# Two graph layers with norms on one core: the step loop of every engine becomes straight code with constant waits

## The reference

```python
def _L0_gnn_ref(input_graph, adj, Wq, bq, Wk, bk, Wv, bv, beta):   # 12 heads of 32
    q, k, v = split(x @ Wq + bq), split(x @ Wk + bk), split(x @ Wv + bv)
    scores = einsum('bhqd,bhkd->bhqk', q, k) / sqrt(HD) + beta * adj
    scores = where(adj > 0, scores, -9e15)
    return merge(einsum('bhqk,bhkd->bhqd', softmax(scores), v))

def layer(h, params):                                              # two of these
    u = einsum('bid,bjd->bij', h, h) / sqrt(D)
    delta = softmax(u) * adj
    attn = delta / (sum(delta) + 1e-10)
    hl, hs, hr = h @ wl.T + b_l, h @ ws.T + b_s, h @ wr.T + b_r
    ctx = (attn * upper) @ hl + diag(attn) * hs + (attn * lower) @ hr
    return relu((ctx - mean) / sqrt(var + 1e-12) * g + beta)

x = layernorm(x + attention(x, adj))
x = layernorm(x + layer(layer(x)))
```

## Time and profile before

| | |
|---|---|
| median of 3 runs | 1378.46 us (1377.25 to 1379.92) |
| profiled execution, its own time | 1381.73 us |
| span of that execution (first to last instruction) | 1380.0 us |
| granted clock of TensorE, mean over the span | 0.982 of full speed |
| PE busy | 1313.9 us, 95% |
| DVE busy | 1057.1 us, 77% |
| ACT busy | 757.1 us, 55% |
| POOL busy | 597.1 us, 43% |

### The profile page before, as it was taken

One profiled execution on the slowest core, in us unless ns is written; L12 is line 12 of the kernel. 1 busy time (PEld: TensorE's weight loads), 2 busy tenths in 40 slices (PEclk: granted clock), 3 DMA queues, 4 the chain that ended last, 5 costly groups with the idle time before them and its releaser, 6 DMA issues.

```text
span 1380.0 us, 37486 instructions
## 1 busy us (share of the span) xinstructions
PE 1313.9 (95%) x13568; PEld 1289.9 (93%) x13568; DVE 1057.1 (77%) x2665; ACT 757.1 (55%) x1579; POOL 597.1 (43%) x656
## 2 busy tenths in 40 slices
PE   3799999999999999999999999999999999999895
PEld 3799999999999999999999999999999999999884
DVE  3358877878877888887787887788888778787765
ACT  4355555565555565555555555556555556555553
POOL 1344444444444444444444445444444444444432
PEclk9799999999999999999999999999999999999997
DMA  7210111110011111011111011111101111101000
GB/s 243 78 40 2 51 51 52 52 50 19 30 50 50 50 50 40 9 50 50 50 50 50 19 31 50 50 50 50 39 11 50 50 50 50 50 15 26 25 13 24
DMA packets 49445, 62.74 MB, mean 45 GB/s; under 512 B 14320, under 2 KB 35952, under 8 KB 49392
## 3 DMA queue, kind: packets, MB, share of 16 engines
q1 hardware_dynamic: 49392, 62.03, 14.7%
HBM read 36.44 MB, written 12.58 MB: 36 GB/s over the span
## 4 chain that ended last, share of the span: by engine, by line
PE 94%; DMA 2%; issue 1%; DVE 1%; ACT 1%; POOL 0%; SPq 0%; POOLq 0%; ACTq 0%
PE bank L315 26%; PE bank L317 25%; PE bank L316 25%; PE bank L427 4%; PE bank L393 4%; PE bank L378 3%; PE bank L364 3%; PE bank L414 2%; PE bank L404 2%; DMA late<-in_w 2%; PE bank L455 1%; ACT w_hi L520 0%; DVE ln_six L841 0%; DVE w_lo L683 0%; ACT late L621 0%
## 5 line engine op out<-in xcount | busy, mean ns | idle before, releaser
L315 PE MATMUL bank<-w_hi,hT_hi 128*128 128x384 f32 x1152 | 403.0, 350 | 9.6 <-issue 9.2
L316 PE MATMUL bank<-w_lo,hT_hi 128*128 128x384 f32 x1152 | 390.8, 339 | 0.0
L317 PE MATMUL bank<-w_hi,hT_lo 128*128 128x384 f32 x1152 | 390.6, 339 | 0.0
L997 POOL TENSOR_TENSOR hlr_lo<-late,hlr_hi 128x384 fp32r<-128x384 f32 x256 | 240.5, 940 | 245.8 <-ACT hlr_hi L596 244.4
L596 ACT ACTIVATE hlr_hi<-late 128x384 fp32r<-128x384 f32 x256 | 134.5, 526 | 222.3 <-DVE late L798 220.4
L315 PEld LDWEIGHTS bank<-w_hi,hT_hi 128*128 128x128 f32 x1152 | 217.2, 189 | 15.3 <-issue 12.4
L798 DVE TENSOR_TENSOR late<-bank,rows 128x384 f32<-128x384 f32 x256 | 142.1, 555 | 101.9 <-PE bank L317 97.9
L316 PEld LDWEIGHTS bank<-w_lo,hT_hi 128*128 128x128 f32 x1152 | 217.6, 189 | 0.0
L317 PEld LDWEIGHTS bank<-w_hi,hT_lo 128*128 128x128 f32 x1152 | 217.1, 188 | 0.0
L1010 POOL TENSOR_TENSOR ln_rstd<-ln_var,minus_half 128x2 f32<-128x2 f32 x128 | 98.7, 771 | 225.1 <-DVE ln_var L867 117.4
L315 PE MATMUL bank<-xT_hi,w_hi 128*128 128x256 f32 x576 | 164.6, 286 | 8.4 <-ACT kT L535 8.4
(11 more groups left out here) (93 smaller groups left out, 2804.7 us busy)
## 6 DMA issues: line engine op xcount, KB each, us to landing
v_halves<-v_stage SPq DMA_DIRECT2D x128, 99.0 KB, 2.3
xT_in<-in_xT SPq DMA_DIRECT2D x32, 384.0 KB, 3.1
x_in<-in_x SPq DMA_DIRECT2D x32, 384.0 KB, 3.8
out<-late SPq DMA_DIRECT2D x32, 384.0 KB, 2.4
late<-in_w SPq DMA_DIRECT2D x9, 576.0 KB, 6.1
adj_in<-in_adj SPq DMA_DIRECT2D x32, 64.0 KB, 3.5
adjT_in<-in_adjT SPq DMA_DIRECT2D x64, 32.0 KB, 2.9
rows<-in_bl SPq DMA_DIRECT2D x2, 192.0 KB, 6.2
```

What stands on the lines that cost most here:

```text
L315: nc.tensor.matmul(o, l_hi, r_hi, start=n == 0, stop=False)
L316: nc.tensor.matmul(o, l_hi, r_lo, start=False, stop=False)
L317: done = nc.tensor.matmul(o, l_lo, r_hi, start=False, stop=n == last)
L997: nc.gpsimd.tensor_tensor(hlr_lo[:, t, m, 0:D], hlr[:, t, m], hlr_hi[:, t, m, 0:D].bitcast(F32), ALU.subtract).then_inc(hlrlo_ready, 1)
```

## The change

All 35 steps are emitted one after the other on every engine; there is no loop, no register and no branch. Each wait is for a constant. The helper `need_alone` is replaced by `need`, so the extra waits on `consts_set` are gone; SyncE's wait on `v_staged`, which the loop body left out, now stands in every step. The arithmetic, the order of the operations on each engine and all buffers are the same.

```diff
-    def __init__(self, it, par):
-        self.it, self.par, self.fixed = it, par, isinstance(it, int)
+    def __init__(self, s):
+        self.s = s
...
     def count(self, stage, per, k):
 
-        const = (self.par + stage) * per + k
-        if self.fixed:
-            value = 2 * self.it * per + const
-            return value if value > 0 else None
-        assert LOOP_FROM * per + const > 0
-        return self.it * (2 * per) + const
+        value = (self.s + stage) * per + k
+        return value if value > 0 else None
...
-def steps(nc, engine, emit):
-    for s in range(-STAGES_BEFORE, LOOP_FROM):
-        emit(Step(s // 2, s % 2))
-    with nc.Fori(LOOP_FROM // 2, LOOP_TO // 2, engines=(engine,), hint_back_edge=True) as it:
-        emit(Step(it, 0))
-        emit(Step(it, 1))
-    for s in range(LOOP_TO, UNITS + STAGES_AFTER):
-        emit(Step(s // 2, s % 2))
+def steps(emit):
+    for s in range(-STAGES_BEFORE, UNITS + STAGES_AFTER):
+        emit(Step(s))
...
-        def need_alone(eng, st, sem, value):
-
-            if not st.fixed:
-                eng.wait_ge(consts_set, 1)
-            need(eng, sem, value)
...
                 if st.has(EARLY):
 
-                    if st.fixed:
-                        need(sp, v_staged, st.count(EARLY, 2, 2))
-                    need_alone(sp, st, o_scaled, st.count(MID, 2, 2))
+                    need(sp, v_staged, st.count(EARLY, 2, 2))
+                    need(sp, o_scaled, st.count(MID, 2, 2))
```

More of the change, by code:

```diff
@@ L9 @@
 ACT = mybir.ActivationFunctionType
-ENG = mybir.EngineType
 AX_X = mybir.AxisListType.X
@@ L41 @@
 class Step:
-    def __init__(self, it, par):
-        self.it, self.par, self.fixed = it, par, isinstance(it, int)
+    def __init__(self, s):
+        self.s = s
     def has(self, stage):
-        return not self.fixed or 0 <= 2 * self.it + self.par + stage < UNITS
+        return 0 <= self.s + stage < UNITS
     def unit(self, stage):
-        return self.it * 2 + (self.par + stage)
+        return self.s + stage
     def slot(self, stage):
-        return (self.par + stage) % 2
+        return (self.s + stage) % 2
     def count(self, stage, per, k):
-        const = (self.par + stage) * per + k
-        if self.fixed:
-            value = 2 * self.it * per + const
-            return value if value > 0 else None
-        assert LOOP_FROM * per + const > 0
-        return self.it * (2 * per) + const
-    def dma_count(self, stage):
[L67 to L72, removed]
-    def count_pair(self, stage):
[L76 to L80, removed]
+        value = (self.s + stage) * per + k
+        return value if value > 0 else None
+    def dma_count(self, stage):
+        value = 16 * ((self.s + stage) // 2 + 1)
+        return value if value > 0 else None
+    def count_pair(self, stage):
+        value = 32 * ((self.s + stage) // 2 + 1)
+        return value if value > 0 else None
 def need(eng, sem, value):
@@ L249, in load_xT @@
             def load_xT(st, ahead):
-                need_alone(sp, st, xlo_ready, st.count(ahead - 2, 1, 1))
+                need(sp, xlo_ready, st.count(ahead - 2, 1, 1))
                 slot = st.slot(ahead)
@@ L255, in load_x @@
                 slot = st.slot(ahead)
-                need_alone(sp, st, x_added, st.count(ahead - 2, 2, 2))
+                need(sp, x_added, st.count(ahead - 2, 2, 2))
                 sp.dma_start(x_in[:, slot], x[st.unit(ahead)]).then_inc(x_loaded[slot], 16)
@@ L283, in step @@
             def step(st):
-                if st.fixed and st.unit(EARLY) == 0:
+                if st.unit(EARLY) == 0:
                     for n in range(RAW, NW):
@@ L291, in step @@
                 if st.has(FINAL):
-                    need_alone(sp, st, y_ready, st.count(FINAL, 2, 2))
+                    need(sp, y_ready, st.count(FINAL, 2, 2))
                     sp.dma_start(out[st.unit(FINAL)], c1).then_inc(y_stored, 16)
                 if st.has(EARLY):
-                    if st.fixed:
-                        need(sp, v_staged, st.count(EARLY, 2, 2))
-                    need_alone(sp, st, o_scaled, st.count(MID, 2, 2))
+                    need(sp, v_staged, st.count(EARLY, 2, 2))
+                    need(sp, o_scaled, st.count(MID, 2, 2))
                     for g in range(GRAPHS):
@@ L303, in step @@
                             sp.dma_start(dst, src.rearrange("p t h d -> p t (h d)")).then_inc(v_moved, 16)
-            steps(nc, ENG.SP, step)
+            steps(step)
             sp.wait_ge(y_stored, 16 * UNITS)
@@ L435, in project_sides @@
             def project_sides(st, l):
-                if st.fixed and st.unit(LATE) == 0 and l == 0:
+                if st.unit(LATE) == 0 and l == 0:
                     pe.wait_ge(w_hi_set, NW)
@@ L507, in step @@
                     mix(st, 1)
-            steps(nc, ENG.PE, step)
+            steps(step)
         @block.scalar
@@ L673, in step @@
                     scale_self(st, 1)
-            steps(nc, ENG.Activation, step)
+            steps(step)
         @block.vector
@@ L691, in stats @@
                 for t in range(T):
-                    need_alone(dve, st, s_six, st.count(stage, per, k + t + 1))
+                    need(dve, s_six, st.count(stage, per, k + t + 1))
                     nc.vector.bn_aggr(mv[:, t], six[:, t]).then_inc(s_mv, 1)
@@ L716, in make_add @@
                 need(dve, adj_loaded[slot], st.dma_count(MID))
-                if st.fixed and st.unit(MID) == 0:
+                if st.unit(MID) == 0:
                     dve.wait_ge(cols_in, 80)
@@ L842, in stats_inner @@
                 for t in range(T):
-                    need_alone(dve, st, s_six, st.count(stage, 2, t + 1))
+                    need(dve, s_six, st.count(stage, 2, t + 1))
                     nc.vector.bn_aggr(mv[:, t], six[:, t]).then_inc(s_mv, 1)
@@ L933, in step @@
                     self_bias(st, 1)
-            steps(nc, ENG.DVE, step)
+            steps(step)
         @block.gpsimd
@@ L1037, in step @@
                     sides_low(st, 1, 1)
-            steps(nc, ENG.Pool, step)
+            steps(step)
 _SHAPE = (B, N, D)
```

1 line of the change is left out of this document (removed).

## The result

| | before | changed |
|---|---|---|
| median of 20 runs each, us | 1378.89 (1376.77 to 1380.72) | 1375.65 (1373.37 to 1376.86) |
| ratio | | 0.9977, 95% interval 0.9970 to 0.9984 |
| span of the profiled execution, us | 1380.0 | 1373.9 |

The changed kernel is faster by 0.23% (0.16% to 0.30%), 3.2 us of the 4.55 forecast. Of the changed kernel's page these lines answer to the earlier trace rows; the columns are the same.

The account below looks back on a forecast made before the run. PE, busy for 95% of the span, was taken to bound the kernel. Back edge 2.29, step 28 1.81 and step 29 0.45 sum to 4.55 us, off a median of 1378.46: 1373.9 us, range 1371.2 to 1377.8.

Parts of the forecast that it names:

- The back edge: Loop steps 4 to 27: POOL's late `xT_lo` holds up DVE, then PE; straight code gives back 2.29 us.
- The exit: Steps 28 and 29: engines leaving the loop reach code not yet fetched; without a loop 1.81 and 0.45 us go.
- Late fetches: Straight code from step 6 on adds about 124 fetch packets; cost between 0 and 87 us, taken as near 0.
- Costed at nothing: Register instructions inside the steps, waits on `consts_set` and SyncE's new wait for `v_staged`: claimed to cost no time.
- The slower rival: Steps 28 and 29 show straight code's true face, with late fetches throughout steps 4 to 27; 1403 us, chance 0.09.
- C: The slower rival's letter in the prediction: late fetches are the way of straight code; 1403 us, chance 0.09.

Follow-up runs that it names:

- the control: The kernel before, unchanged, run once more against itself; ratio 1.0006 (0.9997 to 1.0016).
- the shifted one: The changed kernel with 48 more instructions of satisfied waits at the start of PE's program; ratio to the kernel before 0.9975 (0.9963 to 0.9988).
- the version without that wait: The changed kernel with `make_add` moved behind `hT_low` and `max_gram` on DVE; medians 1368.94 and 1367.35 us, ratios to the kernel before 0.9938 and 0.9912.

## Why the prediction came out as it did

**The direction, the place and the shape** were right. The time of 1375.65 lies in the range of 1371.2 to 1377.8, and the gain is 0.7 of the forecast. A little of the closeness is luck: the forecast stood on a median of 1378.46 from three runs, and twenty runs gave 1378.89, which took 0.4 us off the miss.

**The back edge, 2.29 us.** The two traces of the loop give 979.25 and 979.02, the two of straight code 977.20 and 977.09, so 2.0 us: the term was 0.3 too large. The mechanism was right in its main part: `xT_lo` late, DVE behind it, PE behind DVE. The run with `make_add` late shows it, since the price vanishes with the loop still in place. Incomplete was my account of why `xT_lo` is late. I named POOL's register wait alone. It is 0.09 of the 0.15 us; the other 0.06 is ACT's back edge ahead of `xT_hi`. That the lateness passes on one for one is what the rows show: `xT_lo` 0.15 us later, PE's idle time 0.16 us longer.

**The exit, 1.81 + 0.45 = 2.26 us.** This is the term that was mis-sized. That it belongs to the exit and goes as a whole is shown (the loop to step 16, PE alone, ACT and DVE alone). Its size was read from one execution. Against 40.71 it is 2.26 there, 1.29 in the control, and 1.72 where the loop ends at 16. The mean of the three is 1.76. The run on POOL alone, which left the exit as it was, has 1.89, and the two loops with `make_add` late have 1.90 and 1.75 over their own steps. The prediction read the largest of six. Where the surplus lies is seen too: PE's gap in the scores was 1.02 us there and 0.47 to 0.75 in the others, and DVE's gap of 0.25 us in step 29 is in two traces (before, and POOL alone) and absent in the control, with PE alone and in step 17 of the loop to 16. The reading of step 28 was also incomplete. The two idle times make 1.51 of the 1.81 us; the other 0.3 is PE's busy time, 41.01 for 40.51, less the usual wait of 0.21 before the first product, which falls away.

**Late fetches.** I put their cost near 0, and it is: 0.05 + 0.16 us in one trace, and in the other a delay of 0.08 that a wait took up. I had no account of where they come: at one place in every fifth step. The count of q8 was 109 for 107; that of q14 was 55 for 70, since the three steps that I scaled up from held more of its packets than their share.

**The sum again**, from both traces of each kernel: steps 4 to 29 last 1062.93 and 1061.73 with the loop, 1058.63 and 1058.52 without, so 3.1 to 4.4 us and 3.8 in the mean. The first 20 runs of each give 3.2 us (2.2 to 4.1 by the interval), the second session of the changed kernel 0.18% (2.5 us), the shifted one 0.25% (3.4 us). The 3.8 us lie inside the intervals of the first and the last and just above that of the second (1.2 to 3.6 us); no run separates the steps from the times more finely than that. The larger difference of the two spans came from outside the changed steps, as the control showed.

**Costed at nothing**: the register work on PE (PE alone as straight code leaves the even steps at 40.88), the waits on `consts_set`, and SyncE's extra wait on `v_staged` (steps 4 to 29 are as short as steps 1 to 3, which always had it).

**The slower rival** (1403 us) needed straight code to run short of instructions as steps 28 and 29 did. The loop to step 16 has ten straight steps in a row at 40.71. Its grain of truth is the late fetch, which cost 0.5 us at most in a step and came in at most two steps of a run at a visible price.

The rule of the Trainium skill that I set against C (Runtime: NRT & Kernel Launch, Instruction fetch mechanics), that a taken branch breaks the fetch in sequence, fits the body of four steps, where PE stood idle for 0.14 to 0.62 us behind each back edge; with the body of two steps the back edge brought no packet at all. The same section of the Trainium skill calls the cost of crossing a block of code mostly hidden. That holds here: of the 109 packets of PE all but a few cost nothing, late ones are in part taken up by PE's wait for `hT_lo`, and in the version without that wait 0.3 to 0.5 us of a late fetch shows.

## What to carry to other kernels

A loop on the engines cost little by itself here. Look for what starts first behind the back edge and whether anything on the bounding engine's path waits for it. Here moving two small DVE instructions behind `hT_low` gave 8 to 9 us with the loop kept (medians 1369.46 for 1378.28 and 1370.01 for 1378.47), where writing the loop out gave 3. Before a gap seen once is put into a sum, see whether a second trace has it at the same size: the steps of the loop repeated to 0.2 us in 979, the exit only to 1 us in 2.

## What the runs showed of the hardware that I had not expected

- A DVE instruction of 0.22 us took 1.27 to 1.43 us while POOL's `xT_lo` ran, and 0.23 us at another place. The step's length hung on it through a third engine, PE.
- A loop body of two steps stays on PE and is never fetched again (34 packets on q8 in all); with four steps it is fetched in every round (117 packets), more than with no loop at all (109).
- Leaving a loop cost PE 0.4 to 1.0 us of idle time in the scores, and ACT 1.1 to 1.4 us before `aT_hi`, the latter 39 us after ACT's branch in the trace before (1205.54 to 1244.39), so an engine can pay for the exit long after it. PE's share goes with the end of the first packet on q8 behind the branch (0.99 us into step 28 and a gap of 0.47 in the control, 1.45 and 1.02 in the trace before). Why that packet ends later in one execution than in another stays open.
